# A decoder layer on one core: the self attention's weight tiles turned two heads at a time, and spread onto the block diagonal by two copies of half the partitions

## What is computed

```python
x = x + attn(layernorm(x))            # here: x is (16, 64, 256)
q, k, v = (xn @ (codes * scales) + b for each of wq, wk, wv)   # 256 -> 2048
scores = einsum('bqhd,bkhd->bhqk', q, k) / sqrt(128)           # 64 x 64 per sequence and head
attn = softmax(scores, axis=-1)
out = einsum('bhqk,bkhd->bqhd', attn, v).reshape(B, S, 2048)
return out @ (wo_codes * wo_scales) + bo                       # 2048 -> 256
x = x + xattn(layernorm(x), ctx)      # untouched
x = x + moe(layernorm(x))             # untouched
```

## Time and profile before

| | |
|---|---|
| time of the kernel before, median of 3 runs | 593.21 us (593.02 to 594.74) |
| profiled execution: span from first to last instruction | 581.0 us |
| its own time beside the span | not listed; the median is 12.2 us above the span |
| PE busy | 543.3 us, 94% of the span |
| DVE, ACT, POOL busy | 406.2, 251.6, 209.5 us |
| self attention in the trace | from about 13 us to 228 us |
| mean granted TensorE clock | 0.993 of full speed |

### The profile page before, as it was taken

The page is one execution under the profiler, slowest core; times in us unless marked ns, Lnnn a source line. Parts: engine busy times, 40 slices in busy tenths (PEclk is TensorE's granted clock), DMA queues, the critical chain, the costliest instruction groups (busy, mean ns, idle before and its releaser), DMA issues.

```text
span 581.0 us, 10223 instructions
## 1 busy us (share of the span) xinstructions
PE 543.3 (94%) x3713; PEld 448.2 (77%) x3713; DVE 406.2 (70%) x938; ACT 251.6 (43%) x517; POOL 209.5 (36%) x177
## 2 busy tenths in 40 slices
PE   6989999999999999999999999999988799999891
PEld 5779989898889889666667676667877678999781
DVE  6788895516664576977777765789955599665673
ACT  2454553636463553002013212356463588565451
POOL 8955341030100020332552233012777534444442
PEclk9999999999999999999999999999999999999997
DMA  8235104005030049993000000610272684356433
GB/s 298 78 151 186 39 0 183 1 1 190 1 137 2 2 163 341 332 333 135 0 1 2 0 1 0 237 57 0 74 264 101 180 289 127 119 164 190 145 95 110
DMA packets 21808, 68.65 MB, mean 118 GB/s; under 512 B 4139, under 2 KB 12115, under 8 KB 20724
## 3 DMA queue, kind: packets, MB, share of 16 engines
q1 hardware_dynamic: 16508, 55.17, 28.3%
q0 software_dynamic: 3792, 8.43, 4.0%
q10 hardware_dynamic: 1460, 4.40, 2.5%
HBM read 58.51 MB, written 28.48 MB: 150 GB/s over the span
## 4 chain that ended last, share of the span: by engine, by line
PE 67%; DVE 18%; DMA 5%; issue 5%; ACT 3%; POOL 2%; SPq 1%; DVEq 0%; POOLq 0%; ACTq 0%
PE psum L696 10%; PE psum L565 8%; PE psum L617 5%; PE psum L630 4%; PE psum L762 4%; PE psum L578 4%; DMA yv<-parts_of_tokens 3%; PE psum L718 3%; PE psum L712 2%; PE psum L884 2%; PE psum L714 2%; PE psum L733 2%; PE psum L609 2%; PE psum L753 2%; PE psum L596 2%
## 5 line engine op out<-in xcount | busy, mean ns | idle before, releaser
L1293 DVE TENSOR_TENSOR tt<-psum,tab 128x512 f32<-128x512 f32 x96 | 60.3, 680 | 23.1 <-PE psum L696 22.1
L1635 POOL TENSOR_TENSOR rp<-tt,tt 128x512 f32<-128x512 f32 x24 | 30.8, 1284 | 96.7 <-DVE tt L1293 96.7
L1669 POOL DMA_INDIRECT parts_of_tokens<-yb,xg x39 | 40.5, 1039 | 55.9 <-ACT yb L1117 42.8
L884 PE MATMUL psum<-EW,xgh 128*128 (+1 forms) x188 | 56.7, 344 | 0.1
L565 PE MATMUL psum<-xTh,W 128*128 128x512 f32 x128 | 51.7, 404 | 1.5 <-DVE W L1195 0.8
L565 PE MATMUL psum<-xTl,W 128*128 128x512 f32 x128 | 50.7, 396 | 0.0
L1262 DVE TENSOR_TENSOR OTl<-psum,OTh 128x512 fp32r<-128x512 f32 x32 | 22.2, 693 | 40.8 <-ACT OTh L983 40.7
L1017 ACT ACTIVATE qP<-psum 128x512 f32<-128x512 f32 x16 | 8.7, 595 | 75.3 <-PE psum L718 75.3
L696 PE MATMUL psum<-xTh,Ah 128*128 128x512 f32 x96 | 40.1, 418 | 0.0
L1569 POOL TENSOR_TENSOR rst<-bst,half 128x1 f32<-128x1 f32 x24 | 13.5, 575 | 68.5 <-DVE bst L1154 66.9
L696 PE MATMUL psum<-xTh,Al 128*128 128x512 f32 x96 | 38.0, 396 | 0.0
(11 more groups left out here) (258 smaller groups left out, 1564.4 us busy)
## 6 DMA issues: line engine op xcount, KB each, us to landing
rows_of_experts<-in_empty SPq DMA_DIRECT2D x8, 2064.0 KB, 32.1
exr<-in_ex SPq DMA_DIRECT2D x9, 608.0 KB, 7.3
xg<-rows_of_experts SPq DMA_DIRECT2D x39, 129.0 KB, 2.2
exr<-in_ex ACTq DMA_DIRECT2D x7, 608.0 KB, 5.4
yv<-parts_of_tokens SPq DMA_DIRECT2D x8, 512.0 KB, 4.6
raw<-in_codes SPq DMA_DIRECT2D x6, 512.0 KB, 6.3
raw<-in_codes SPq DMA_DIRECT2D x3, 1024.0 KB, 7.9
wor<-in_woc SPq DMA_DIRECT2D x4, 512.0 KB, 3.4
```

Of the source, the lines that this page charges most:

```text
L884: mm = pe.matmul(ap[:, 0:352], xp[b % 2][:, 128 * kt:128 * kt + 128], piece(b, o + 352 * kt, 352), start=(k == 0), stop=(k == 5))
L1293: return tt_(b3(tt[n][:, :], 64), b3(src, 64), tab[:, j % 3, n, :].unsqueeze(1).to_broadcast([128, 8, 64]), ALU.mult)
L1635: tt_(o[:, 0, :], tt[0][:, :], tt[1][:, :], ALU.subtract).then_inc(s_rp_lo, 1)
L1669: nc.gpsimd.indirect_dma_start(out=parts_of, out_offset=to, in_=yb[b % 4][:, :], in_offset=None, bounds_check=4 * 1024 - 1, oob_is_err=Fal ...
```

## The change

In the scores, the partitions now hold two heads (`odd` 0 and 1 of a pair) of one sequence and the columns run over pair and sequence; there are as many matmuls, of the same shapes. `Pb` is [128, 16, 64] and full, without zeros. A row's sum, inverse and product are as before in size, but the product is one DVE instruction on 128 partitions for each half, in block 7 as well, and POOL's part of block 7 is gone. A turn is two transposes instead of four: each turns a 128 x 128 tile (two heads one above the other in the partitions, two sequences beside each other in the columns) into one with sequences in the partitions and heads in the columns. ACT writes this to the block diagonal of `PT` in two instructions, partitions 0 to 63 and 64 to 127, each with 256 elements in a partition in place of one instruction with 512. The zeros around the diagonal are now in `PT`; POOL writes them by two memsets behind the rotation of the context, and its memset of `Pb` at the start is gone. ACT waits for these memsets before its first turn, where it waited for `kv2`.

```diff
@@ tensor_program @@
             def scores(c):
-                    for h in range(4):
-                        col = 256 * (i % 2) + 64 * h
-                        for half_ in range(2):
-                            o = 128 * i + 64 * half_
-                            mm = pe.matmul(sides[n][0][64 * half_:64 * half_ + 64, col:col + 64],
-                                           qT[:, h, o:o + 64], kT[:, h, o:o + 64], start=True, stop=True)
+                    for pair in range(2):
+                        for batch in range(2):
+                            o = 128 * i + 64 * batch
+                            col = 256 * (i % 2) + 128 * pair + 64 * batch
+                            for odd in range(2):
+                                h = 2 * pair + odd
+                                mm = pe.matmul(sides[n][0][64 * odd:64 * odd + 64, col:col + 64],
+                                               qT[:, h, o:o + 64], kT[:, h, o:o + 64], start=True, stop=True)
             def turn(c, i):
...
-                for h in range(4):
-                    mm = pe.transpose(ap[:, 128 * h:128 * h + 128], Pb[:, 4 * i + h, :], ident[:, :])
+                te.wait_ge(s_pb, 2 * c + i // 2 + 1)
+                for p in range(2):
+                    mm = pe.transpose(ap[:, 128 * p:128 * p + 128],
+                                      Pb[:, 4 * i + 2 * p:4 * i + 2 * p + 2, :].rearrange("p h k -> p (h k)"), ident[:, :])
@@ scalar_program @@
             def turn(c, i):
                 sc_.wait_ge(*ps.filled("turn", c, i))
-                if c == 0:
-                    sc_.wait_ge(s_kv2, 2)
+                sc_.wait_ge(s_ptz, 2)
...
-                act(PT[i % 2][:, :], ps.of("turn", c, i), ACT.Copy).then_inc(ps.drain("turn", c, i), 1)
+                src = ps.of("turn", c, i)[:, 0:256].rearrange("p (a b s) -> p a b s", a=2, b=2)
+                dst = PT[i % 2][:, :].rearrange("p (a b s) -> p a b s", a=2, b=4)
+                act(dst[0:64, :, 0:4:2, :], src[0:64], ACT.Copy)
+                act(dst[64:128, :, 1:4:2, :], src[64:128], ACT.Copy).then_inc(ps.drain("turn", c, i), 1)
@@ vector_program @@
             def probs(c):
...
-                    ve.wait_ge(s_pbz, 1)
...
-                    for q in range(1 if c == 7 else 2):
-                        lo, hi = 64 * q, 64 * q + 64
-                        op = tt_(Pb[lo:hi, g, lo:hi], m3[lo:hi, g, :],
-                                 rs[lo:hi, g].unsqueeze(2).to_broadcast([64, 8, 64]), ALU.mult)
-                    op.then_inc(s_pb, 1)
+                    tt_(Pb[:, g, :], m3[:, g, :], rs[:, g].unsqueeze(2).to_broadcast([128, 8, 64]),
+                        ALU.mult).then_inc(s_pb, 1)
@@ gpsimd_program @@
-            nc.gpsimd.memset(Pb[:, :, :], 0.0).then_inc(s_pbz, 1)
...
             def context():
...
+                for i in range(2):
+                    nc.gpsimd.memset(PT[i][:, :], 0.0).then_inc(s_ptz, 1)
...
-            def probs(c):
-                if c == 7:
...
```

More of the change, by code:

```diff
@@ L426, in program @@
         V = at("V", R3 + 16384, [128, 4, 512])
-        Pb = at("Pb", R3 + 24576, [128, 16, 128])
+        Pb = at("Pb", R3 + 24576, [128, 16, 64])
         PT = [at(f"PT{i}", R3 + 32768 + 2048 * i, [128, 512]) for i in range(2)]
@@ L473, in program @@
         ps = Banks(psum, sem)
-        s_ident, s_half, s_kvz, s_pbz = (sem(n) for n in ("ident", "half", "kv_zero", "pb_zero"))
+        s_ident, s_half, s_kvz, s_ptz = (sem(n) for n in ("ident", "half", "kv_zero", "pt_zero"))
         d_x, d_cst, d_kvr = [sem("x0_in"), sem("x1_in")], sem("bias_in"), sem("kv_in")
@@ L495, in program @@
         s_mx, s_exp, s_sum, s_rs = sem("row_max"), sem("exp"), sem("row_sum"), sem("row_inverse")
-        s_pb, s_pb_pool = sem("probs"), sem("probs_by_pool")
+        s_pb = sem("probs")
         s_ot_hi, s_outs, s_x2, s_xb = sem("ot_hi"), sem("outs"), sem("x2"), sem("x_bias")
@@ L1328, in cross_scores @@
                     ve.wait_ge(s_pb, 16)
-                    ve.wait_ge(s_pb_pool, 2)
                 elif t <= 3:
@@ L1672, in gpsimd_program @@
             part = {"norm": norm, "context": context, "weights_qk": weights_qk, "weights_v": weights_v,
-                    "weights_wo": weights_wo, "probs": probs, "bias": bias, "rotate": rotate, "split13": split13, "split2": split2,
+                    "weights_wo": weights_wo, "bias": bias, "rotate": rotate, "split13": split13, "split2": split2,
                     "low": low, "scatter": scatter, "block_down": block_down}
```

## The result

The changed kernel takes 589.14 us (median of 6 runs, 588.21 to 590.88), the kernel before, run beside it, 593.21 us (6 runs, 591.55 to 594.74). By the medians that is 4.1 us less (ratio 0.9931). The ratio on record is 0.9916, 95% interval 0.9898 to 0.9935, which is 5.0 us of 593.21, with 3.9 to 6.1 as its ends. Either is beyond the 0.3% that can be told from no change, and both fall short of the 6.7 us that were forecast: 589.14 is 2.6 us above 586.5, and 0.2 above the upper end of the range, 588.9; the ratio on record gives 588.2, which is inside.

What follows compares the result with a forecast made beforehand. PE was taken to bound the kernel from block 3 to about 228 us, other engines at a few places. Turns 6.1, block 0 0.5, `kT` 0.2, block 7 -0.1, start 0 sum to 6.7 us: 593.2 to 586.5 us, range 584.8 to 588.9.

Steps and rivals of the forecast that it cites:

- The turns' price: PE's turns: 0.109 us a transpose, each turn loses two, 0.218 us; 6.1 us over all blocks.
- the scores at 2.02 us: PE's scores: taken as unchanged at 2.01 us; rival that they lose their overlap and the kernel gets slower, 4%.
- PE's wait for `kT` in block 2 gone: Block 2: PE's 0.2 us wait for DVE's `kT` goes, gaining 0.2 us.
- no wait for `PT` outside block 7: Blocks 1 to 6: ACT's copies leave 0.14 us of slack at values 0; rival that they become the bound, 12%.
- block 7's loss ahead of values 0: Block 7, first values: ACT's pair of `PT` copies ends 0.08 later, a loss of 0.1 us.
- The gain passed through behind 228 us: Behind the self attention: no work edited, gain passes through in full; rival that it is given back, 9%.
- In block 0 the mechanism held: Block 0: POOL's memsets delay `W`, which holds the first `Pb` to 35.87; `kT` still ends earlier, PE gains 0.5 us.
- In blocks 1 to 6 all four turns count.: PE in blocks 1 to 6: every turn's saving shortens the chain, 6 x 0.87 = 5.2 us.
- DVE in blocks 1 to 6 ... everywhere but in block 2 it was early enough: DVE gets 1.38 us shorter in each of these blocks; it matters only in block 2, at `kT`, worth 0.2 us.
- Block 7's other two turns: Block 7, turns 2 and 3: their savings count, 0.44 us; the first two only lengthen PE's wait.
- The pair of half copies: ACT's two 256-column `PT` copies: 0.68 us for the pair, upper end 1.08, against about 0.60 for one of 512.
- the prediction's three: Start, order of `xh` and POOL's `W`: gain 1.2 us (15%), about even, or loss 0.7 (20%); taken as 0.

Runs made afterwards that it cites:

- the two comparisons: Unaltered changed kernel against the kernel before: 589.14 us against 593.21 (ratio 0.9916), and again on another chip 588.45 against 593.34 (ratio 0.9913).
- the runs with `W` out of the way: Changed kernel with POOL's `PT` memsets behind its v weights of the second block, 574.9 us; another with POOL's first `W` waiting for all four `xh`, 575.61 us.
- the `V` first kernel: Changed kernel with ACT's copy of the next block's first `V` ahead of `OTh` in blocks 0 to 6: 576.62 us, before 581.06, ratio 0.9913.

## Why the prediction was right and where it was short

**Right.** The turns' price (0.109 us a transpose; chain at 0.44 and 0.22), the scores at 2.02 us, PE's wait for `kT` in block 2 gone, no wait for `PT` outside block 7, and block 7's loss ahead of values 0: the turns came to values 0 in 1.38 us before (213.07 to 214.45) and in 1.48 now (208.46 to 209.94), the forecast 0.1. The gain passed through behind 228 us: 4.77 there, 4.1 and 4.9 at the end by the medians of the two comparisons (5.0 and 5.2 by the ratios on record). In block 0 the mechanism held: `Pb` was held until 0.54 behind `W` (0.55 in the prediction). That it ended at 35.87 to the hundredth is luck: POOL's memsets took 0.53 us each, not 0.45, and POOL came to them 0.18 earlier. Behind `Pb` the way to the end of `kT` was 0.94 us shorter (2.23 in place of 3.17), not 0.69, so values 0 came 0.74 earlier, and less the 0.19 of the start that is the 0.55 of the table. The Trainium skill ("SBUF — State Buffer", section "Who interferes with whom") states that a DVE instruction with two SBUF inputs, such as `Pb` and `xh`, and a GpSimd instruction that reads SBUF exclude each other, and the runs with `W` out of the way (`Pb` 1.04 us shorter, `xh` at 0.48) agree with it.

**Step that failed: "In blocks 1 to 6 all four turns count."** Three do. Turn 2 stands between values 0 and v(c+1, 1), and the latter wait for the bank that ACT empties only after `OTh`: from 107.54 to 109.81, 2.27 us of latency, whatever PE does in it. PE's own work there was 2.22 (0.89, 0.44, 0.89) and is 2.00. Before, values 0 to v took 2.23 us (110.12 to 112.35) and the copy of `V` ended at 112.30, so the latency stood right at PE's heels, and no wait showed. I had looked for slack only in front of values 0, behind ACT's `PT`. It cost 0.22 to 0.26 us in each of blocks 0, 1 and 3 to 6 and 0.1 in block 2, about 1.6 us in all. Doubling turn 2 for nothing and paying for turn 3 shows it. (From block 2's turns on the table has the 1.07 of the forecast all the same: that is luck, since the stretch from the turns to values 0 gained 0.74 there and not 0.64.)

**Step that failed: "DVE in blocks 1 to 6 ... everywhere but in block 2 it was early enough", and that in block 2 only `kT` was late.** There a chain outside PE reaches from block 1's second values to block 2's qk, and it gained 1.05 us, not PE's 1.55. It begins on ACT, behind the values of block 1:

```profile
63.66 0.59 ACT L961 ACTIVATE V<-psum 128x512 f32<-128x512 f32 x1
...
64.52 0.38 ACT L979 ACTIVATE PT<-psum 64x256 f32<-64x256 f32 x1
64.92 0.60 ACT L984 ACTIVATE OTh<-psum 128x512 fp32r<-128x512 f32 x1
```

From `V` to the next `OTh` it is 1.26 us; before it was 0.95 (65.01 to 65.96), with one copy between them. There 0.31 us of a gain of 1.35 went. `OTl` and `V` on DVE follow (66.17, before 67.22), then the layer norm's statistics and `sclB`, and with `sclB` POOL's `W`, which holds DVE's two `xh`:

```profile
70.55 4.59 POOL L1590 TENSOR_TENSOR W<-raw,sclB 128x2048 fp32r<-128x2048 f32 x1 [1.62 <-DVE sclB L1189]
72.21 3.60 DVE L1168 SCALAR_TENSOR_TENSOR xh<-xs,bst,rst 128x256 f32<-128x256 f32 x2
```

Before, `W` began at 71.63 and the `xh` ended at 76.90; now they end at 75.81, though DVE came to them 1.57 us earlier. What DVE had gained beyond `W`'s 1.08 went into a longer hold (3.60 in place of 3.12 us). Behind `xh` stand `sclB`, `xTl`, `mx` and `sm`, behind these ACT's `exp` and `qT`, each 1.04 to 1.09 earlier than before, and PE's qk matmul, 1.55 earlier until then, waits:

```profile
81.67 0.50 PE L565 MATMUL psum<-xTh,W 128*128 128x512 f32 x1 [0.22 <-ACT qT L949]
```

0.48 us of the gain ended there. The ACT part is shown: with overlapping copies (128 partitions, spread columns) `V` to `OTh` took 1.01 us, DVE's `V` came at 65.66, `W` at 70.06, `xh` ended at 75.33, and 0.25 was gained from block 1's turns to scores 3. The part of `W` was read from the trace; no run takes it away at this place.

**Sizes.** Block 7's other two turns gave 0.26 in place of 0.44. Turn 3 was worth its 0.22; from turn 2 to the end of values 1 it was 1.33 before (216.72 to 218.05) and is 1.27 (212.21 to 213.48), and doubling turn 2 made block 7 only 0.05 longer. What takes its saving there no run isolates. The pair of half copies measures 0.77 us (0.39 + 0.38), not 0.68: the row I took it from has copies on all partitions, which overlap. It cost the 0.1 in block 7 and the 0.3 ahead of block 2, at a copy that the prediction didn't look at. PE's first turn waited 0.29 us for `Pb`, not 0.1 at most, which cost nothing, since values 0 waited for `kT` behind it. The start came out nearly even (0.19), as taken, but by luck and in a way that isn't among the prediction's three: the third `xh` slipped in ahead of `W` and the fourth was held by it, as in the kernel before, and ended at 11.26. In two other profiles the start lost 1.5 us (last section), twice the 0.7 that the range allowed for.

## What to carry to other kernels

Work taken out of the busiest engine counts only where no chain through another engine spans it: for each edit, take the stretch between the last release and the next wait on that engine, and compare its own work with the latency of that chain (a list of waits can't show that the slack is only 0.01 us: no wait is there until the work is taken out). Doubling the removed piece is a quick test of whether it counts: here turn 2 against turn 3. And an instruction that could run early but stands behind one that waits, as `V` behind `OTh`, is worth moving, or giving to another engine, before any work is removed.

## What the runs showed of the hardware that was not expected

- Two ACT copies of 256 columns in a row start 0.26 to 0.29 us apart when both use all 128 partitions, and 0.38 to 0.39 apart (no overlap; each lasts 0.38) when the first uses partitions 0 to 63 and the second 64 to 127. The change of partitions alone doesn't explain it. In the changed kernel the half copy behind `V`, which uses all partitions (109.16, 0.59 us long), overlaps it by 0.11 us, and `OTh`, on all partitions, doesn't overlap the half copy ahead of it:

```profile
109.64 0.37 ACT L978 ACTIVATE PT<-psum 64x256 f32<-64x256 f32 x1
110.02 0.38 ACT L979 ACTIVATE PT<-psum 64x256 f32<-64x256 f32 x1
110.43 0.60 ACT L984 ACTIVATE OTh<-psum 128x512 fp32r<-128x512 f32 x1
```

In the kernel with copies on all partitions `OTh` follows such a copy after 0.26 us (64.13 to 64.39). So it is behind a copy of half the partitions that the overlap is missing here. No run has two copies in a row on the same half, and the cause stays open.

- At the start the order of POOL's first `W` and DVE's third `xh` falls either way: in seven of the nine profiles whose start has the code of the changed kernel the `xh` came first, in two `W`. In the `V` first kernel `W` began at 9.11, ahead of it, and the third and fourth `xh` were each held by a `W`:

```profile
8.59 3.68 DVE L1168 SCALAR_TENSOR_TENSOR xh<-xs,bst,rst 128x256 f32<-128x256 f32 x4
9.11 2.88 POOL L1590 TENSOR_TENSOR W<-raw,sclB 128x512 fp32r<-128x512 f32 x2
10.92 0.34 PE L552 MATMUL psum<-ident,xh 128*128 128x128 f32 x1 [0.97 <-DVE xh L1168]
12.33 0.48 PE L552 MATMUL psum<-ident,xh 128*128 128x128 f32 x1 [0.86 <-DVE xh L1168]
```

In the changed kernel it began at 9.44 and the four `xh` took 2.67 us. What follows is more than the late `xh`. From 12 to 20 us the windows (PE, PEld, DVE, ACT, POOL busy, granted clock, DMA share, GB/s) are, changed, then `V` first:

```profile
12.00:20.00 8.00, 7.73 (x36) 6.15 (x35) 5.71 (x9) 4.59 (x8) 6.35 (x5) 1.00 0.68 267
```

```profile
12.00:20.00 8.00, 7.67 (x27) 6.54 (x28) 6.68 (x12) 2.45 (x4) 4.74 (x3) 0.63 0.65 258
```

In finer windows the clock was 1.00 up to 11.0 us, 0.50 from 11.5 to 16.0, the level of 1.2 GHz, and 1.00 (2.4 GHz) again from 18.0 on; the first 32 qk matmuls took 9.01 us in place of 7.74. It fell behind the first of the two gaps shown, not behind both: a transpose at 11.09 already lasted 0.38 us in place of 0.27. The last two gaps ahead of the fall were of 0.66 us (until 9.12) and 0.97 (until 10.92). The changed kernel's profile has 1.27 (until 9.12) and 0.97 (until 11.32), that of the kernel before 1.43 and 1.07, and both kept 1.00, so the length of the gaps alone doesn't tell when the clock falls; what does stays open. The first qk came 1.5 us later (14.38), scores 1 2.4 us (53.48). It was so in two profiles, this one and that with turn 2 doubled. In the three kernels with `W` behind the fourth `xh` the first qk came at 11.82 to 11.90.
